# Attention and a mixture of experts on one core: the maxima of two heads read by one VectorE instruction, and four small products made one

## The reference

```python
attn = softmax(einsum('bhid,bhjd->bhij', q, k) / sqrt(16))     # 8 batches, 16 heads, 512 x 512
coh  = sigmoid(tanh(concat(x, c) @ Wc1.T + bc1) @ Wc2.T + bc2) # one gate for each row and head
mod  = attn * coh;  mod = mod / (mod.sum(-1) + 1e-8)
mod  = (1 - 0.21) * mod + 0.21 * fa                            # fa: one weight for each column
x    = x + (einsum('bhij,bhjd->bhid', mod, v) @ Wout.T + bout)
x    = x + experts(x)                                          # gates, top 2, three layers each
```

## Time and profile before

| | us |
|---|---|
| median of 3 runs | 939.65 (936.78 to 946.73) |
| the profiled execution's own time | 950.3 |
| its span, from the first to the last instruction | 948.4 |
| first and last read of a maximum (L1320) begins at | 32.9 and 502.7 |
| DVE busy in it | 699.8 (74%) |
| PE busy in it | 878.1 (93%) |

### The profile page before, as it was taken

One profiled execution on the slowest core, in us unless ns is written; L12 is line 12 of the kernel. 1 busy time (PEld: TensorE's weight loads), 2 busy tenths in 40 slices (PEclk: granted clock), 3 DMA queues, 4 the chain that ended last, 5 costly groups with the idle time before them and its releaser, 6 DMA issues.

```text
span 948.4 us, 23132 instructions
## 1 busy us (share of the span) xinstructions
PE 878.1 (93%) x6806; PEld 514.9 (54%) x6807; DVE 699.8 (74%) x1680; ACT 581.5 (61%) x1256; POOL 406.3 (43%) x446
## 2 busy tenths in 40 slices
PE   5799999999999999998888989799999999999994
PEld 2232333333333333332231678678888888888873
DVE  6768889888998988989996387768865555555442
ACT  3147877877778878787586657655444444444441
POOL 4313435555646656553253326643553233223322
PEclk9679999999999999999896899989999999999998
DMA  6543243443526426171053187875644333333432
GB/s 207 121 80 71 66 53 91 97 113 79 97 82 109 122 60 127 42 124 48 13 173 114 26 243 179 192 191 100 129 74 57 46 57 52 51 46 55 66 49 25
DMA packets 109434, 88.36 MB, mean 93 GB/s; under 512 B 63816, under 2 KB 102216, under 8 KB 107024
## 3 DMA queue, kind: packets, MB, share of 16 engines
q1 hardware_dynamic: 95664, 68.05, 31.6%
q0 software_dynamic: 13296, 18.23, 11.6%
q10 hardware_dynamic: 384, 0.93, 0.3%
HBM read 44.97 MB, written 33.31 MB: 83 GB/s over the span
## 4 chain that ended last, share of the span: by engine, by line
PE 74%; DVE 11%; ACT 5%; DMA 4%; issue 3%; POOL 1%; SPq 1%; DVEq 0%; ACTq 0%; POOLq 0%
PE bank L1053 30%; PE bank L950 10%; PE bank L898 10%; PE bank L1069 9%; PE bank L885 8%; DVE mx L1320 5%; PE bank L874 4%; ACT arena L1203 2%; PE bank L956 2%; DVE arena L1627 1%; DMA w_b<-mxp 1%; PE bank L1008 1%; DMA out<-y,y_dest 1%; POOL arena L654 1%; ACT arena L1151 1%
## 5 line engine op out<-in xcount | busy, mean ns | idle before, releaser
L1320 DVE TENSOR_REDUCE mx<-bank 128x1 f32<-128x512 f32 x512 | 324.3, 682 | 49.2 <-PE bank L874 46.1
L1203 ACT ACTIVATE arena<-bank 128x512 f32<-128x512 f32 x512 | 277.4, 596 | 70.4 <-PE bank L885 68.5
L1239 ACT ACTIVATE hf<-bank,small 128x256 f32<-128x256 f32 (+1 forms) x312 | 133.5, 456 | 190.2 <-PE bank L1053 188.3
L753 POOL DMA_INDIRECT out<-y,y_dest x71 | 130.5, 1838 | 239.5 <-DVE y_dest L1608 207.8
L1053 PE MATMUL bank<-hh,arena 128*128 128x256 f16 (+1 forms) x1248 | 198.6, 265 | 0.1
L874 PE MATMUL bank<-arena 48*128 48x512 f16 x512 | 170.8, 396 | 16.8 <-DVE mx L1320 12.8
L1589 DVE TENSOR_TENSOR hl<-hf,hh 128x256 f16<-128x256 f32 (+1 forms) x304 | 112.6, 395 | 93.7 <-ACT hh L1243 93.2
L885 PE MATMUL bank<-arena 49*128 49x512 f16 x512 | 164.5, 394 | 14.6 <-DMA arena<-w_b 6.3
L1053 PE MATMUL bank<-hl,arena 128*128 128x256 f16 (+1 forms) x624 | 163.6, 263 | 0.0
L898 PE MATMUL bank<-arena 128*17 128x512 f32 x1024 | 139.6, 618 | 0.9 <-ACT arena L1203 0.9
L885 PEld LDWEIGHTS bank<-arena 49*128 49x128 f16 x512 | 39.1, 94 | 177.5 <-ACT arena L1203 149.2
(11 more groups left out here) (228 smaller groups left out, 971.3 us busy)
## 6 DMA issues: line engine op xcount, KB each, us to landing
raw<-in_we SPq DMA_DIRECT2D x16, 1024.0 KB, 5.2
arena<-parts_dram SPq DMA_DIRECT2D x84, 128.0 KB
parts_dram<-arena SPq DMA_DIRECT2D x64, 128.0 KB, 1.8
arena<-in_xT SPq DMA_DIRECT2D x8, 512.0 KB, 4.5
arena<-in_x SPq DMA_DIRECT2D x8, 512.0 KB, 5.9
out<-rows SPq DMA_DIRECT2D x8, 512.0 KB, 5.2
xs<-in_pads SPq DMA_DIRECT2D x9, 272.0 KB, 3.6
arena<-parts_dram SPq DMA_DIRECT2D x24, 64.0 KB, 3.0
```

The lines of the kernel that those rows point to most:

```text
L753: pool.indirect_dma_start(out=out, out_offset=bass.IndirectOffsetOnAxis(ap=y_dest[:, par, s:s + 1], axis=0), in_=y[:, par, s, :], in_offse ...
L1203: nc.scalar.activation(pr[:, s % TT, n, :], b_bank[no % B_RING][:, :], ACT.Exp, scale=SCALE).then_inc(b_read, 1)
L1239: nc.scalar.activation(hf[which][:, m, 0:n], layer[which][m // 2][:, m % 2 * TS:m % 2 * TS + n], ACT.Relu, bias=bias[which][:, bass.ds(e, ...
L1320: V.tensor_reduce(mx[:, g % 2, c, s % TT:s % TT + 1], a_bank[no % A_RING][:, :], X, ALU.max).then_inc(a_read, 1)
```

## The change

The three banks become one PSUM tensor `scores`. Of a slot's four maxima the first two are read by one instruction over two neighbouring banks (`reduce_pair`), the other two each by one as before. So that the pair lies in neighbours, the banks go by slot: in even slots a0 to a3 take banks 1, 0, 2, 0, in odd slots 2, 1, 0, 2. a3 therefore takes a bank that the pair of its own slot has to have left; a0 and a1 wait for the read of a2 of the slot before, a2 for that of a3 of the slot before. `a_read` counts three reads a slot instead of four. The four coherence products of a batch (places 0 to 3) become one task at place 2, of eight matmuls into one bank, and one evacuation of 64 columns.

```diff
-A_RING, B_RING = 3, 2
+B_RING = 2
+A_BANKS = ((1, 0, 2, 0), (2, 1, 0, 2))
+PAIR_BANKS = (slice(0, 2), slice(1, 3))
+A_READS = 3
...
-    0: [("coh", 0, 0), ("v", 0, 1)],
-    1: [("coh", 1, 0), ("ot", 3, -1)],
-    2: [("at", 1, -1), ("coh", 2, 0)],
-    3: [("coh", 3, 0), ("op", 0, -1)],
+    0: [("v", 0, 1)],
+    1: [("ot", 3, -1)],
+    2: [("at", 1, -1), ("coh", 0, 0)],
+    3: [("op", 0, -1)],
...
         def a_tile(s, n):
-            at, par, no = s % TT, s // SLOTS % 2, s * G + n
-            if no >= A_RING:
-                pe.wait_ge(a_read, no - A_RING + 1)
+            at, par = s % TT, s // SLOTS % 2
+            if n == 3:
+                pe.wait_ge(a_read, A_READS * s + 1)
+            elif s > 0:
+                pe.wait_ge(a_read, A_READS * s - (0 if n == 2 else 1))
...
-            nc.tensor.matmul(a_bank[no % A_RING][:, :], q[r, par, h // 2, at * P:(at + 1) * P], k[r, par, h // 2, :],
+            nc.tensor.matmul(a_bank[A_BANKS[s % 2][n]][:, :], q[r, par, h // 2, at * P:(at + 1) * P], k[r, par, h // 2, :],
                              start=True, stop=True).then_inc(a_ready, 1)
...
             elif what == "coh":
-                for e in range(ET):
-                    last = nc.tensor.matmul(m[:, 0:H], hT[:, e, i * P:(i + 1) * P], w["wc2"][:, e, :],
-                                            start=(e == 0), stop=(e == ET - 1))
+                for t2 in range(TT):
+                    for e in range(ET):
+                        last = nc.tensor.matmul(m[:, t2 * H:(t2 + 1) * H], hT[:, e, t2 * P:(t2 + 1) * P], w["wc2"][:, e, :],
+                                                start=(t2 == 0 and e == 0), stop=(e == ET - 1), skip_group_check=True)
...
+        def reduce_pair(s):
+            g = s // TT
+            dve.wait_ge(a_ready, s * G + 2)
+            V.tensor_reduce(mx[:, g % 2, 0:3:2, s % TT], score_banks[:, PAIR_BANKS[s % 2], :], X, ALU.max).then_inc(a_read, 1)
...
             elif what == "coh":
                 after(dve, ez_ready, b)
-                V.tensor_tensor(z[:, i, :], m[:, 0:H], w["bc2"][:, :], ALU.add).then_inc(done, 1)
+                V.tensor_tensor(z[:, :, :], m[:, 0:TT * H].rearrange("p (t h) -> p t h", t=TT),
+                                w["bc2"][:, None, :].to_broadcast([P, TT, H]), ALU.add).then_inc(done, 1)
...
             if scored(s + LEAD):
-                reduce_head(s + LEAD, 0)
-                reduce_head(s + LEAD, 1)
+                reduce_pair(s + LEAD)
```

More of the change, by code:

```diff
@@ L118, in sb @@
             return ctx.enter_context(nc.sbuf_tensor(name, shape, dt))
-        banks = [ctx.enter_context(nc.psum_tensor(f"bank{i}", [P, 512], F32)) for i in range(8)]
+        scores = ctx.enter_context(nc.psum_tensor("scores", [P, 3, 512], F32))
+        banks = [ctx.enter_context(nc.psum_tensor(f"bank{i}", [P, 512], F32)) for i in range(3, 8)]
         xs = nc.dram_tensor("xs", [NX * CAP + TS, ROW], F32).ap()
         parts_dram = nc.dram_tensor("parts_dram", [2, 2 * E, S], F16).ap()
-        model(nc, ctx, dram, sb, banks, xs, parts_dram, out)
+        model(nc, ctx, dram, sb, scores, [scores[:, i, :] for i in range(3)] + banks, xs, parts_dram, out)
 def shaped(flat, shape):
@@ L291, in results_of, with model @@
     return 16 * (SUB * min(tiles, LARGE // 2) + max(tiles - LARGE // 2, 0))
-def model(nc, ctx, dram, sb, banks, xs, parts_dram, out):
+def model(nc, ctx, dram, sb, score_banks, banks, xs, parts_dram, out):
     def sem(name):
@@ L773, in _ @@
             if at == 4 and 0 <= b < B:
-                evicted(pool, ("coh", TT - 1, b))
+                evicted(pool, ("coh", 0, b))
                 nc.gpsimd.tensor_scalar(z[:, :, :], z[:, :, :], -88.0, None, ALU.max).then_inc(z_ready, 1)
@@ L1102, in _ @@
             if s == FINAL + 14:
-                pe.wait_ge(a_read, B * SLOTS * G)
+                pe.wait_ge(a_read, A_READS * B * SLOTS)
                 hold_ranks(0, EARLY)
@@ L1314, in chain @@
             dve.wait_ge(link, n_link[0])
+        def reduce_pair(s):
+            g = s // TT
+            dve.wait_ge(a_ready, s * G + 2)
+            V.tensor_reduce(mx[:, g % 2, 0:3:2, s % TT], score_banks[:, PAIR_BANKS[s % 2], :], X, ALU.max).then_inc(a_read, 1)
         def reduce_head(s, n):
[L1317 to L1320, removed]
+            g, c = s // TT, column(head_of(n, True))
+            dve.wait_ge(a_ready, s * G + n + 1)
+            V.tensor_reduce(mx[:, g % 2, c, s % TT:s % TT + 1], a_bank[A_BANKS[s % 2][n]][:, :], X, ALU.max).then_inc(a_read, 1)
         def split_maxima(g):
-            dve.wait_ge(a_read, (g + 1) * TT * G)
+            dve.wait_ge(a_read, (g + 1) * TT * A_READS)
             if g >= 2:
```

## The result

| | before | the change |
|---|---|---|
| median of the runs, us | 942.59 (936.78 to 946.73, 4 runs) | 976.32 (973.2 to 979.59, 4 runs) |
| ratio to before | | 1.0363 [1.029, 1.0436] |
| the profiled execution's own time, its span | 950.3, 948.4 | 973.2, 971.1 |
| last read of a maximum begins at | 502.7 | 531.3 |

What follows compares the result with a forecast made beforehand. In attention PE and DVE were both close to full, PE leading in most slots. Terms of 0.64 + 0.58 + 0.74 + 0.68 = 2.64 us a batch, times seven, gave 18 us slower: 958 us, range 940 to 972.

Steps and rivals of the forecast that it cites:

- The pair's price (1.22): On DVE, one read of 1024 columns takes 1.22 us against 1.29 for two reads; upper end 1.36.
- a3's start in a slot where PE leads: At place 1, a3 can start 1.73 us after a1, so PE loses 0.21 us in the slot.
- PE's waits as the sign: If right, PE's wait for reads grows from 44.6 us to 60 or more.
- the small terms by place: Attention's losses and gains per batch at groups of its 16 places, summing to 2.64 us a batch.
- Rival 1: DVE is the bound, so fewer reads and evacuations make the kernel faster: 13 us gained, 927 us; chance 0.13.
- rival 2: The waits are absorbed by ACT or DVE's gains and coherence is neutral: 944 us, or 940; chance 0.19.
- rival 3: Slower still: pair takes 1.36, 967 us; coherence in one piece keeps ACT waiting for b tiles, 969; chance 0.13.
- the slope: On DVE, a maximum's time grows 1.05 ns a column from 64 to 512 columns.
- place 3 ... gains 0.46 and loses about 0.08: Place 3 of a batch loses its 0.46 us coherence product and pays about 0.08, counted as -0.38.
- seven batches have this pattern: The loss of 2.64 us a batch was multiplied by seven, giving 18 us; the last batch was left out.
- 2.64: Forecast loss in us per attention batch: 0.64 + 0.58 + 0.74 + 0.68.
- I charge nothing: Last batch, filled by DVE's tables: no loss, since its 0.07 a slot and the waits are of one size.

Runs made afterwards that it cites:

- the pair alone: Kernel before plus only the paired read and new order of banks; the four coherence products stand apart as before: 974.53 us, 1.0317.
- the short pair: Paired read and its banks without the coherence change, the pair reading 256 columns of each bank instead of 512: 938.66 us, 0.9937.
- the coherence alone: Kernel before plus only the coherence of a batch as one product; reads, banks and waits as before: 953.72 us, 1.011.
- the coherence in two: The change with the coherence of a batch as two products of four matmuls, at places 0 and 2, and two evacuations: 973.24 us, 1.031.

## Why the prediction was right, and where it was wrong

**Right.** The pair's price (1.22), a3's start in a slot where PE leads (T + 1.94 forecast, 1.96 measured), PE's waits as the sign, and the small terms by place, in the steady batches: places 8, 9, 14 and 15 forecast 0.64, measured 0.63; 6 and 7, 0.58 and 0.74; 10 to 13, 0.74 and 0.71; 0, -0.34 and -0.32; 1 and 2 together, +1.40 and +1.46; 4 and 5, 0 and 0.01. In places 1 and 2 two errors cancel, which is luck: place 1 gained 0.22 where nothing was said, and place 2 lost 1.68 where 1.40 was said, because a3 there did not come "in time" but waited for the pair until T + 2.49 (before T + 1.82) and put the tasks off. That the waits cost time is shown by the pair alone and by the four single reads with the change's waits, at clock 1.00 in batches 1 to 5 of both. Rival 1 (DVE the bound) is out, since fewer reads on DVE went with more idle time ahead of them; rival 2 (absorbed) too, and of rival 3 neither half came in as I had it, the 1.36 not at all. The Trainium skill (Perfetto Trace Analysis, Optimizing Scalar/DVE Operations) says that smaller instructions may let work finish sooner where the engine isn't saturated but makes others wait. The trace agrees as to the case, with 72.0 us of idle time of DVE against 49.2 and more waits of PE; but smaller instructions alone did not finish sooner, since four single reads under the change's waits took 973.16 us. Grouping the reads saved 0.07 us a slot, two reads of 1.29 us made one of 1.22, and nothing of it is to be seen in the whole time. (That no row of DVE has float32 columns for less than the slope is not so, a memset of 32x4096 took 3472 ns, but the price taken from it held.)

**Wrong: "place 3 ... gains 0.46 and loses about 0.08", and "seven batches have this pattern".** Every price in the sum was taken at clock 1.00, and the sum was multiplied by seven. For batch 1, which ran at 1.00 in both kernels, 2.64 was about right (+1.8 and +2.6). In batches 2 to 5 place 3 did not gain 0.38, it lost 0.94. Places 2 and 3 of batches 1 and 2 of the change side by side:

```profile
122.47:127.56 5.09, 4.73 (x37) 2.86 (x36) 4.26 (x9) 2.93 (x6) 1.95 (x2) 1.00 0.05 10
127.56:130.63 3.07, 3.07 (x24) 1.03 (x24) 2.53 (x4) 2.17 (x4) 0.36 (x1) 1.00 0.69 111
182.63:187.73 5.10, 4.74 (x39) 2.87 (x38) 4.26 (x9) 2.93 (x6) 3.33 (x4) 1.00 0.08 22
187.73:192.13 4.40, 4.40 (x23) 0.92 (x23) 2.37 (x4) 2.04 (x4) 2.98 (x4) 0.61 0.87 172
```

Place 2 is the same in both. Place 3 takes 3.07 at clock 1.00, near the 3.05 that the forecast makes of 3.43 - 0.38, and 4.40 at 0.61. In the timeline of PE, batch 5, from `pv` at place 2:

```profile
367.61 1.05 PE L904 MATMUL bank<-arena 128*17 128x512 f32 x8
...
369.56 0.39 PE L880 MATMUL scores<-arena 48*128 48x512 f16 x1 [0.36 <-DVE mx L1326]
369.88 0.66 PE L962 MATMUL bank<-small,arena 128*128 128x128 f32 x4
370.37 1.90 PE L1015 MATMUL bank<-small,arena 128*128 128x16 f32 x16
...
372.60 0.63 PE L891 MATMUL bank<-arena 49*128 49x512 f16 x1
...
373.16 1.91 PE L904 MATMUL bank<-arena 128*17 128x512 f32 x8
```

Behind a3's wait and 1.90 us of 16-column passes, `pv` takes 1.91 us instead of 1.05, and a tile 0.63 instead of 0.39: TensorE is at 1.2 GHz instead of 2.4. That is 1.3 us a batch that no term held, 5 us over four batches. The block is not its sole condition, since batch 1 has the same block and keeps its clock. Nor is the time to be had back by moving the block: at place 0 there was no half clock in these batches, and they took 61.29 us all the same.

**Not charged at all.** Batch 0 lost 4 us more than 2.64, with the clock down from 0.96 to 0.90, and batch 6 2.7 more, from 0.94 to 0.89. The last batch, where "I charge nothing", lost 3.5 in nine slots, from 0.98 to 0.90; there my argument that waits and gain are of one size failed, and not through the clock alone: with the pair alone the nine slots took 37.53 us at 0.99, 2.3 more than before. Together with place 3 that is the forecast's 18 grown to 33 up to the nine slots' end (6.6 + 1.8 + 16.0 + 5.3 + 3.5). The last step took 10.65 off to come from the profiled execution to the median. That trace of before had a slower rest than that of any changed kernel, so the 10.65 belonged to before and not to the change, whose profiled execution (973.2) lies below its median.

**Open.** What the clock fell for in batches 0 and 6 and not in batch 1. In batch 0 it was 1.00 with the short pair, 0.96 before, 0.90 in the change and 0.83 with the pair alone, but also 0.89 with the coherence alone, where a3 waits for what it waited for before. So the waits of a3 are not its sole condition, and its cause stays open. And the 0.9 us at place 4 with the coherence in two. Of the versions that compute all maxima none beats the kernel before.

## What to carry to other kernels

Before two reads become one, ask which writer needs the first of them: a grouped read gives its banks back together and late, and with three banks in turn the next writer is of the same slot. The 0.07 us that the grouping saves is a third of the 0.21 that the writer loses where PE leads, and a writer that has to wait for two single reads loses as much where DVE is behind. The price of a step in a tuned TensorE order holds for the clock at which it was read: mark where the changed order gives the engine waits or passes of few columns, and put the rows at half clock into the upper end of the range. And moving small products together doesn't shorten them: with the coherence alone the three places that they left gave back 0.91 us (0.45, 0.32 and 0.14), and the one that they came to paid 1.71.

## What the runs showed of the hardware

- Two reads of 512 float32 columns from PSUM, one behind the other, took 1.29 us, one of 1024 columns 1.22. Grouping them saved 0.07 us.
- Place 3 took 4.33 to 4.43 us with half clock and 3.06 without, in four batches of each of two executions of the change; batch 1, with the same instructions on PE, kept its clock. POOL had less to do there (1.95 us in place 2 of batch 1, 3.33 us in that of batch 2), but that is not the sole condition either: with the coherence alone it was batch 1 that had half clock at place 3, and batches 3 to 5 that had none.
- The clock granted in a whole batch repeats from one execution to the next to the second digit in batches 0 to 5 (0.90, 1.00, 0.97 four times; 0.83 and then 1.00 with the pair alone), though not in batch 7 (0.90 and 0.79 in the nine slots). So in these batches it goes with the kernel and not with the execution.
- Two profiled executions of one kernel agreed within 0.6 us and lay 7 to 11 us above the medians of its runs, within their spread (935.99 to 951.52).
